# Preparing the weights of a Mamba and Hadamard-FFN block: where butterfly stages and the first norm are done

## The reference, cut to what matters

```
def fwht(x):
    h = 1
    while h < n:
        x = x.reshape(-1, n // (2 * h), 2, h)
        a, b = (x[:, :, 0, :], x[:, :, 1, :])
        x = jnp.stack([a + b, a - b], axis=2).reshape(-1, n)
        h *= 2
    return x / jnp.sqrt(n)
...
x = fwht(xn * SU_ug) / SCALE
x_up = x @ W_up.T * (Wscale_ug[:INTER] * SCALE)
x_gate = x @ W_gate.T * (Wscale_ug[INTER:] * SCALE)
x = jax.nn.silu(x_gate) * x_up
x = fwht(x * SU_dp) / SCALE
x = x @ W_down.T * (Wscale_dp * SCALE)
...
return x + attn(xn) + ffn(xn)
```

## Time and profile before

| | us |
|---|---|
| three runs, median | 1901.8 (1899.98 to 1902.4) |
| the profiled execution, its own time | 1901.78 |
| its span, first to last instruction | 1900.1 |
| last store of the preparation ends | 188.98 |
| first product of the loop (`bc`) starts | 203.84 |
| from there to the end, 16 blocks | 1696.3 |

### The profile page before, as it was taken

How to read it: one execution, slowest core, us unless ns; L and a number is a source line. 1 busy time by engine, 2 the same in 40 slices (tenths; PEclk the granted TensorE clock), 3 DMA queues, 4 the chain that set the end, 5 groups by cost and what they waited for, 6 DMA issues and landing times.

```text
span 1900.1 us, 40055 instructions
## 1 busy us (share of the span) xinstructions
PE 1783.0 (94%) x13680; PEld 1232.7 (65%) x13682; DVE 1421.7 (75%) x2866; ACT 1228.4 (65%) x2583; POOL 348.7 (18%) x278
## 2 busy tenths in 40 slices
PE   4447799999999999999999999999999999999998
PEld 2124676767586767667676767667675867677675
DVE  6997586867778585868778685868677785858676
ACT  7836575848476665848485765758484766658483
POOL 0440030202112030212121030302021120302121
PEclk9669899999999999999999999999999999999999
DMA  8201113122221313123231313132232313131232
GB/s 317 84 4 56 46 46 84 52 57 79 44 75 36 80 40 87 45 58 77 49 77 38 80 39 79 45 82 54 57 79 38 81 35 80 43 88 45 57 79 56
DMA packets 217572, 125.77 MB, mean 66 GB/s; under 512 B 179662, under 2 KB 180790, under 8 KB 216886
## 3 DMA queue, kind: packets, MB, share of 16 engines
q1 hardware_dynamic: 216870, 122.30, 25.7%
q10 hardware_dynamic: 528, 1.05, 0.2%
HBM read 72.18 MB, written 8.65 MB: 43 GB/s over the span
## 4 chain that ended last, share of the span: by engine, by line
PE 58%; DVE 21%; DVEq 7%; issue 5%; SPq 3%; ACT 3%; DMA 2%; ACTq 1%; PEldq 0%
PE bank L860 55%; DVE rs L1157 2%; DVE rs L1159 2%; DVE wi L592 2%; DVEq L1275 2%; SPq L820 2%; DVE v L1277 1%; DVE Mx L1259 1%; PE bank L653 1%; DVEq L1300 1%; DMA xnT<-cvx 1%; DVE vw L1290 1%; DVEq L1270 1%; DVE h L1232 1%; DVE tg L1228 1%
## 5 line engine op out<-in xcount | busy, mean ns | idle before, releaser
L860 PE MATMUL bank<-xnT,wug 128*128 128x256 f16 x6144 | 699.8, 273 | 0.0
L860 PEld LDWEIGHTS bank<-xnT,wug 128*128 128x128 f16 x6144 | 596.4, 98 | 90.2 <-issue 3.4
L860 PE MATMUL bank<-wd,h 128*128 128x512 f16 x1536 | 360.4, 379 | 4.1 <-DVE h L1232 3.9
L1140 POOL TENSOR_TENSOR state<-state,dec 128x512 f32<-128x512 f32 x64 | 80.1, 1260 | 1005.7 <-ACT neg L1053 731.5
L860 PEld LDWEIGHTS bank<-wd,h 128*128 128x128 f16 x1536 | 148.0, 98 | 168.3 <-DVE h L1232 8.2
L1221 DVE SCALAR_TENSOR_TENSOR cvx<-xc,conv,cvx 128x256 f32<-128x256 f32 x384 | 180.2, 514 | 74.9 <-ACT cvx L1001 65.3
L860 PE MATMUL bank<-wi,xnT 128*128 128x512 f16 (+1 forms) x1152 | 201.7, 330 | 18.8 <-DMA xnT<-cvx 18.5
L1016 ACT ACTIVATE tg<-bank,gate_scale 128x256 f32<-128x256 f32 x256 | 117.3, 471 | 123.8 <-PE bank L860 104.6
L860 PEld LDWEIGHTS bank<-wi,xnT 128*128 128x128 f16 x1152 | 100.9, 99 | 115.7 <-issue 23.6
L860 PE MATMUL bank<-xnT,wi 128*128 128x256 f16 x1536 | 173.1, 273 | 0.0
L1067 ACT ACTIVATE Mx<-Mx,cs_own 128x128 f32<-128x128 f32 x512 | 162.9, 390 | 10.2 <-DMA Mx<-cs_rows 9.7
(11 more groups left out here) (248 smaller groups left out, 2562.3 us busy)
## 6 DMA issues: line engine op xcount, KB each, us to landing
Mx<-cs_rows SPq DMA_DIRECT2D x128, 256.0 KB, 3.6
cvx<-in_L_attn_u_dram SPq DMA_DIRECT2D x17, 512.0 KB, 3.4
Mx<-in_L_attn_u_dram SPq DMA_DIRECT2D x16, 512.0 KB, 3.5
out_dram<-Mx SPq DMA_DIRECT2D x16, 512.0 KB, 3.0
big<-in_L_ffn_W_down_dram SPq DMA_DIRECT2D x2, 2048.0 KB, 11.9
wug<-in_L_attn_in_proj_w_dram SPq DMA_DIRECT2D x2, 2048.0 KB, 12.7
pair<-in_L_ffn_W_gate_dram SPq DMA_DIRECT2D x4, 1024.0 KB, 5.2
pair<-in_L_ffn_W_up_dram SPq DMA_DIRECT2D x3, 1024.0 KB, 5.6
```

The lines of the kernel that those rows point to most:

```text
L860: ins = nc.tensor.matmul(out, lhsT, rhs, start=first and n == 0, stop=last and n == len(pairs) - 1)
L1140: pool.tensor_tensor(half, half, bcast(dec3[:, 2, c, 8 * hf:8 * hf + 8], HD), ALU.mult).then_inc(state_faded, 1)
```

## The change

1. **Up/gate.** `ba` goes away, with the tile `half`. `bb` reads `nat` directly. The stage of stride 128 joins neighbouring units n and n+1, so PE sums it: `H` of an even unit is `had` x `wt[0]` plus `had` x `wt[1]` in one PSUM bank, `H` of the odd one is `had` x `wt[0]` plus `had_neg` x `wt[1]`. Each of the 32 up/gate `H` is two products now; both units of a pair must be copied before the first `H`, and both `H` done before `wt` is written again. The freed half of `pair` is a second load buffer: `nat[g % 2]`.
2. **Down.** POOL's eight instructions go to DVE as `db01` to `db31`. ACT's `dsc` and `dsq` stand earlier.
3. **First block.** The loop's tiles `xin`, `xnT`, `xc`, `ctz`, `stats` and others are laid into `pair`; x is loaded, normed, split and turned inside the preparation: `lna lnb lnc xl0 xl1` stand among the down units in DVE's string, `xh0 xh1` in ACT's, and SP's stream issues load and transposes before `prepared`.
4. All four strings are new; SP's is `wo1 dn0 nat1 dn2 nat2 nat3 in nat4 ...`.

```diff
-wo1 nat1 dn0 nat2 in nat3 dn2 nat4 nat5 nat6 nat7 wo2
+wo1 dn0 nat1 dn2 nat2 nat3 in nat4 nat5 nat6 nat7 wo2
...
-            nat, half = pair[:, 0, :, :], pair[:, 1, :, :]
+            nat = [pair[:, n, :, :] for n in range(2)]
...
                     elif k == "nat":
-                        sp.wait_ge(nat_squared, n)
-                        sp.wait_ge(half_done, n)
+                        if n >= 2:
+                            sp.wait_ge(nat_squared, n - 1)
+                            sp.wait_ge(mixed_done, n - 1)
                         load_group(n)
...
                 sp.sem_inc(prepared, 1)
+                sp.wait_ge(wo_split, CX)
+                sp.dma_start(xin, x_v[0]).then_inc(x_loaded, 16)
+                turn_x(sp, -1)
...
                         if n >= 2:
-                            act.wait_ge(hw_filled, n - 1)
+                            act.wait_ge(hw_filled, (n - 2 | 1) + 1 if n - 2 < UG_UNITS else n - 1)
...
-                        butterfly(half, mixed[n % 2], 2 * P).then_inc(mixed_done, 1)
+                        dve.wait_ge(nat_loaded[n % 2], 16 * (n // 2 + 1))
+                        butterfly(nat[n % 2], mixed[n % 2], 2 * P).then_inc(mixed_done, 1)
...
                     elif k == "H":
-                        pe.wait_ge(wt_copied, n + 1)
                         if n >= 4:
                             pe.wait_ge(hw_stored, n - 3)
-                        nc.tensor.matmul(banks[2 + n % 4][:, :], had[:, :], wt[n % 2][:, :], start=True, stop=True).then_inc(hw_filled, 1)
+                        o = banks[2 + n % 4][:, :]
+                        if n < UG_UNITS:
+                            pe.wait_ge(wt_copied, (n | 1) + 1)
+                            nc.tensor.matmul(o, had[:, :], wt[0][:, :], start=True, stop=False)
+                            nc.tensor.matmul(o, (had, had_neg)[n % 2][:, :], wt[1][:, :], start=False, stop=True).then_inc(hw_filled, 1)
+                        else:
+                            pe.wait_ge(wt_copied, n + 1)
+                            nc.tensor.matmul(o, had[:, :], wt[n % 2][:, :], start=True, stop=True).then_inc(hw_filled, 1)
```

More of the change, by code:

```diff
@@ L92 @@
+T19 sq5 H16 H17 T20 H18 T21 H19 sq6 T22 T23 H20 sq7 H21 T24 T25 H22 H23 H24 H25 T26 T27 H26 T28 H27 T29 T30
+H28 H29 pk T31 wo0 wo1 wo2 H30 wo3 H31 wo4 wo5 T32 T33 wo6 T34 wo7 T35 H32 T36 H33 H34 T37 H35 H36 T38 H37 T39
+T40 H38 T41 H39 T42 H40 T43 xh0 xh1 H41 T44 H42 T45 H43 T46 H44 T47 H45 H46 H47
 """.split()
 PREP_DVE = """
-ba0 bb0 ba1 fs0 bb1 fs1 H0 ba2 bb2 H1 nb0 H2 fs2 db00 H3 H4 ba3 H5 bb3 fs3 nb1 ba4 nb2 H6 bb4 nb3 fs4 H7 nb4
-H8 ba5 H9 nb5 ws bb5 ba6 H10 H11 H12 db10 wi0 fs5 wi1 H13 fs6 wi2 H14 H15 wi3 db20 H16 H17 H18 H19 bb6 ba7 bb7
@@ L96 @@
-H20 H21 H22 fs7 H23 pk H24 H25 H26 db30 H27 H28 H29 H30 wo0 H31 H32 H33 wo1 H34 H35 wo2 H36 wo3 H37 wo4 wo5
-wo6 H38 H39 H40 H41 H42 wo7 H43 H44 H45 H46 H47
+bb0 bb1 fs0 db00 H0 bb2 fs1 H1 nb0 db01 bb3 H2 db10 H3 H4 db11 fs2 nb1 H5 bb4 H6 nb2 H7 db20 nb3 fs3 H8 nb4 H9
+H10 nb5 ws H11 bb5 H12 fs4 wi0 wi1 H13 H14 H15 wi2 wi3 db21 H16 H17 H18 H19 bb6 fs5 bb7 H20 db30 H21 fs6 H22
+H23 H24 H25 fs7 pk H26 H27 db31 wo0 wo1 H28 H29 H30 wo2 H31 wo3 wo4 wo5 wo6 wo7 H32 H33 H34 H35 H36 lna H37
+lnb lnc H38 H39 xl0 xl1 H40 H41 H42 H43 H44 H45 H46 H47
@@ new lines, in program, with halves, rsqrt @@
+        tg_first = space[:, 4096 - TB:4096]
+        def halves(ap, n):
+            return ap.bitcast(F16)[:, 0:n]
+        x_hi = halves(space[:, 8 * TB:8 * TB + XC], NT * DM).rearrange("p (t k) -> p t k", t=NT)
+        x_lo = [halves(xin[:, j, :], DM) for j in range(NT)]
+        def rsqrt(dve, xh, y, a):
+            nc.vector.tensor_scalar(a.bitcast(I32), xh.bitcast(I32), 1, None, ALU.logical_shift_right)
+            dve.drain()
+            nc.vector.tensor_scalar(y.bitcast(I32), a.bitcast(I32), -1.0, RSQRT_SEED, ALU.mult, ALU.add)
+            dve.drain()
+            for _ in range(3):
+                for j in range(xh.shape[-1]):
+                    c = slice(j, j + 1)
+                    nc.vector.tensor_scalar(a[:, c], y[:, c], y[:, c], xh[:, c], ALU.mult, ALU.mult)
+                dve.drain()
+                nc.vector.scalar_tensor_tensor(y, a, 1.5, y, ALU.add, ALU.mult)
+                dve.drain()
@@ new lines, in norm_sums, with norm_root @@
+        def norm_sums(dve, i):
+            dve.wait_ge(x_loaded, (i + 2) * 16)
+            for j in range(NT):
+                nc.vector.bn_stats(stats[:, j, :], xin[:, j, :])
+            dve.drain()
+            for j in range(NT):
+                nc.vector.bn_aggr(mv[:, j, :], stats[:, j, :])
+            dve.drain()
+        def norm_root(dve):
+            nc.vector.tensor_scalar(rs[:, 0, :], mv[:, :, 1], -0.5, -0.5 * LN_EPS, ALU.mult, ALU.add)
+            dve.drain()
+            rsqrt(dve, rs[:, 0, :], rs[:, 1, :], rs[:, 2, :])
@@ L194, in program, with turn_x @@
+        def turn_x(sp, i):
+            for j in range(NT):
+                sp.wait_ge(x_split, (i + 1) * NT + j + 1)
+                sp.sem_inc(turns, 1)
+                sp.dma_start(xnT[:, :, 0, j * P:(j + 1) * P], x_hi[:, j, :], transpose=True).then_inc(xT_loaded, 16)
+                sp.dma_start(xnT[:, :, 1, j * P:(j + 1) * P], x_lo[j], transpose=True).then_inc(xT_loaded, 16)
         with ExitStack() as prep:
@@ L703, in program @@
         ssq = sb("ssq", [P, NT])
[L704 to L711 removed]
+        tg = [tg_first, sb("tg1", [P, TB])]
         y = [[v32[:, 4 * hf:4 * hf + 4, c, :] for hf in range(2)] for c in range(NT)]
```

183 lines of the change are left out of this document (67 added, 116 removed).

## The result

The changed kernel takes **1884.0 us** (median of four runs, 1877.5 to 1886.1) against 1902.1 before: the ratio is 0.9906, 95% interval 0.9893 to 0.9919. It is faster by 0.9%, and the prediction was 1861 with a range of 1852 to 1880. The sign was right, the size was not: more than half of the gain is missing (18.1 us came of 41). The profiled run is one of the four, 1885.27 us, its span 1883.3.

What follows compares the result with a forecast made beforehand. DVE, near full, was taken to bound the preparation, and PE the loop, unchanged at 1696.3 us. From 1901.8, 39.8 for an earlier bc and 0.7 for its clock gave 1861; range 1852 to 1880.

Steps and rivals of the forecast that it cites:

- The step that failed: PE's loop: the change touches none of its order strings, so its 1696.3 us stay.
- Second group: Start of DVE's stretch: second up/gate group arrives at 21.5 us behind the down weights, costing 3.9 us uncovered.
- The stretch on DVE: Preparation, second group's arrival to last store: 171.4 us becomes 147.6 by sum, taken as 142 with fewer waits.
- POOL (-13.6 net): Preparation: DVE gets back 31.3 us lost beside POOL and does 17.7 us more down butterflies.
- The 31.3 lost us: Preparation: time DVE's down butterfly, wi splits and su_scale lose while POOL runs its down butterflies.
- x moved in (+7.0): Preparation: norm and split of the first x add 7.0 us to DVE's work among the down units.
- Tail: End of preparation: x's transposes hidden or late by under 1 us, bc 0.5 us after the last store.
- Clock: First bc on PE: its 24 products took 3.06 us at 1.2 GHz; a warmer clock gains 0.7 us.
- PE as the bound (1882): Up/gate preparation: PE at half rate nearly throughout, bc only 19.2 us earlier; 0.05 shared with DVE's long instructions remaining.
- The rival on DVE's long instructions (1892): Preparation: POOL does not cause them, so 31.3 us stay; 0.05 shared with PE bounding fully.
- The rule that I had set against the change: PE in the preparation: pausing returns it to the slow clock, making PE at half rate the result.
- the one on the slower side: Preparation: PE at half rate to the end, DVE's pk and db31 in series, +14.2 us, 1916; chance 0.03.

Runs made afterwards that it cites:

- experiment 9: Kernel before with one part of the change only: POOL's eight down butterflies done by DVE; 1887.8 us, ratio 0.993.
- experiment 4: Changed kernel without the second product of each up/gate unit, so the butterfly stage of stride 128 is left out; 1854.5 us, ratio 0.9756.
- experiment 2: Kernel before with 256 waits on an already set semaphore (128 instructions) at the start of PE's stream; 1931.8 us, ratio 1.0155.
- experiment 3: Changed kernel with 64 waits on an already set semaphore (32 instructions) at the start of PE's stream; 1886.4 us, ratio 0.992.
- experiment 5: Changed kernel with 64 instructions of already satisfied waits ahead of the third unit's transposes, where PE idles; 1852.5 us, ratio 0.9743.
- experiment 1: Changed kernel with 256 waits on an already set semaphore (128 instructions) at the start of PE's stream; 1862.9 us, ratio 0.980.
- experiment 6: On top of experiment 5, POOL does half of the down butterflies again (8 instructions); 1873.6 us, ratio 0.985.
- experiment 7: On top of experiment 5, the first x is normed, split and turned behind the preparation again; 1866.1 us, ratio 0.982.
- experiment 8: On top of experiment 5, SP loads the second up/gate group ahead of the down weights; 1856.4 us, ratio 0.977.

## Why the prediction was right and wrong

**The step that failed** stands in the first paragraph: the change "touches none of its order strings; its 1696.3 us stay". Its only support was the order of the instructions. The order did stay; the loop's place in PE's stream did not. The sum was 1901.8 - 39.8 - 0.7. Against the profiled runs, `bc` gave 40.4, and the time from `bc` to the end took 23.5 back: +29.8 for seven gaps with their clock (measured above), and -6.3 elsewhere. Of these, 1.4 is the first `bc` at full clock, for which the sum had 0.7; 4.1 is idle time of PE in the rest of the loop, which no step had (by its waits 6.2 us before, 2.1 beside the gaps after); 0.8 isn't placed. The prediction said what would show this premise wrong, a loop outside 1695 to 1697 us, but it gave that no price and no chance, so the range had nothing for it. Had it been a rival, the rows would have priced it only roughly; the shift of the code (32 products at four instructions each) was there to be counted beforehand, and its place in the loop to be asked about.

How far the shift decides, from all runs:

| Instructions on PE ahead of the loop, against before | Kernels | Gaps | Loop from `bc`, us |
|---|---|---|---|
| 0 | before, 9 | none | 1696.3, 1693.3 |
| 0 (the added products left out) | 4 | none | 1690.4 |
| 128 | after; 2 | 7, behind 25 products | 1719.8; 1720.4 |
| 160 | 3 | 7, behind 10 products | 1722.6 |
| 192 | 5 | none | 1690.7 |
| 256 | 1 | none | 1692.5 |

6, 7 and 8 have 5's padding and no gaps either. PE's records bear the shifts out: 779 stand ahead of the loop before, 908 after, 973 in experiment 5, give or take a missing one, and a turn has 3462 in all kernels. With 25 products to the edge, PE outruns the fetch and waits; with 128 instructions more to it, as before, the fetch lands in time. That a shift of 256 gives the same picture as one of 0, and that packets are 16 KB, agrees with the block size that the Trainium skill states (the same section, "Instruction fetch mechanics"); that the fetch is "mostly hidden", as it says of crossing an edge, holds here behind a branch only where enough code of the block is left.

**What held, term by term.**

- *Second group:* forecast 21.5, measured 20.90. But the opinion that its lateness costs 3.9 us was wrong: experiment 8 took it away and lost 3.0.
- *The stretch on DVE:* forecast 142 us, measured 162.0 - 20.9 = 141.1. That is the 147.6 of the sum less 6.5 of waits.
- *POOL (-13.6 net):* in the kernel before alone, 11.2 us on `bc` (experiment 9); in the changed one 17 (experiment 6). The 31.3 lost us of the earlier trace rows were read right as durations. What they are worth on the path depends on what else waits.
- *x moved in (+7.0):* its real price was 2.4 (experiment 7), since the tail had waits for ACT to fill. That the sum of 142 came out has a share of luck in it: I had taken the waits of the tail away and charged x in full, and the two go together; in the changed kernel 3.1 us of the 4.1 for ACT's `wd` are still there.
- *Tail:* the last store to `bc` took 1.5 us, forecast 0.5; `bc` waited there for DVE's drain (the `DVEq L1346` of its row). The transposes were issued by 160.13, before the last store ended, as said.
- *Clock:* 3.06 became 1.67 us, a gain of 1.4; I took 0.7. Experiment 7 brings the 3.06 back with an idle PE ahead.

**The rivals.** PE as the bound (1882) gives nearly the measured time, and for the wrong reason: experiment 4 takes 32 products away and `bc` moves by 1.9 us, by 0.6 against experiment 5. Reading the time alone, one would have called this rival right. The granted clock of 20 to 160 us is 0.94 in experiment 5 and 0.83 with the products left out: with more to do PE was not slowed to the half rate but was at the full one for more of the stretch. The rule that I had set against the change, from the Trainium skill, "TensorE: Matmul & The Clock Gate", section "The HAM clock gate" (a PE that keeps pausing goes back to the slow state), did not decide here, although PE still pauses. The rival on DVE's long instructions (1892) falls by experiments 6 and 9, the one on the slower side with experiment 4.

**What stays open.** Without gaps the loop takes 1689.6 to 1692.5 us in the kernels with the new layout (1, 4 to 8) and 1693.3 to 1696.3 in those with the old one. About half of this spread is idle time of PE in front of its loop's products: by its waits 6.2 us in the kernel before, 4.2 in 9, and 4.0, 3.5, 2.6, 2.3, 1.1 and 1.5 in 1, 4, 5, 6, 7 and 8. Less these, the loops take 1686.9 to 1690.1 us. What is left, and why PE waits less, I can't name. Nor is it settled why the second packet starts 5.9 to 6.3 us behind the branch in the changed kernel and 5.5 to 5.8 in experiment 3, or why one of the changed kernel's runs was 1877.5 us and the others 1882.8 to 1886.1 (a turn that comes out of its gap at full clock is 1.7 us shorter, and in experiment 2 three of seven did; which did in that run isn't on record). A shift between 192 and 256, or one that leaves 60 to 170 instructions to the edge, wasn't tried, so the point from which the gap is hidden is known only to lie between 50 and about 178 instructions (50 plus 128). An estimate from the packets: the code is there 3.4 to 4.7 us after `bc` starts (second packet plus 2.3), and by then PE has done 24 products in 1.5 us and one more every 0.11 us, so some 80 to 110 instructions.

## What to carry to other kernels

Where an engine's loop has thousands of instructions a turn (3462 on PE here), an instruction added ahead of the loop can move the places at which it waits for code; look for `<- issue` gaps at one fixed instruction of every turn, and try a shift by 64 or 128 instructions, laid where the engine idles anyway. Here that was worth 31.6 us (1884.0 to 1852.5), more than the 18.1 that the change itself had gained; the kernel before took 1902.1 beside the first and 1900.6 beside the second. And price each premise of the form "this part stays as it is": here the largest term was the one that wasn't in the sum.

## What the runs showed of the hardware

- A turn of PE's loop can cost a gap for code (2.5 to 2.9 us in the changed kernel), and 4.3 us on average with the half clock that follows it (29.8 over seven turns); the same code shifted by 64 instructions costs nothing.
- Behind every taken branch of PE's loop two packets of 16 KB follow, the first after 0.9 to 1.8 us, the second after 4.7 to 6.7. PE's stream stands for 3.3 to 4.3 us at the first, hidden by products still running, and all 21 gaps end 2.2 to 2.8 us after the second starts.
- A float32 product of 512 columns counts as four instructions on PE (128 for 32).
- A wait on a semaphore that is already set is not free on PE: 256 of them are 128 instructions, and in experiment 1 they start 0.11 us apart, from 1.79 to 15.60 us. Some 5 us of that lie in time in which PE had nothing to do anyway, so its first product moved from 7.09 to 15.71. Placed in PE's idle time, 64 instructions moved `bc` no later.
- Next to POOL, DVE's butterflies, `wi` splits and `su_scale` are stretched, the small one too (`su_scale` of 128x4: 0.23 us alone, 3.50 beside POOL, ending with POOL's instruction). A store that reads a PSUM bank kept its 0.74 us (experiment 6). POOL's own instructions, 4.5 us each at best, took up to 6.55 beside DVE in the kernel before. With POOL back in the changed kernel, 41.0 us of POOL's work stretched DVE's by 19.2 and added 15.5 of idle time.
